# Query and key stacks transposed by DMA instead of by TensorE, in an attention and expert kernel on one Trainium2 core

## The reference

```
h = einsum('bhid,oi,od->bho', x, weighted_sum, weight)      # the mix: 512 x 256 per batch
h = h + attention(layernorm(h))                             # 16 heads of 16
h = h + experts(layernorm(h))                               # 8 dense experts, 256 -> 1024 -> 256, relu,
                                                            # weighted by sigmoid gates over 0.5
attention: q, k, v = split(t @ qkv_w.T + qkv_b); q, k = rotate(q), rotate(k)
           q = q / max(norm(q), 1e-12); k = k / max(norm(k), 1e-12)     # per head
           out = softmax(q k^T / 4) v;  return out @ out_w.T + out_b
```

## Time and profile before

| what | value |
|---|---|
| median of 3 runs | 2000.3 us (1999.42 to 2002.72) |
| the profiled execution, its own time | 1997.95 us |
| its span, first to last instruction | 1996.2 us |
| PE / ACT / DVE / POOL busy | 95% / 57% / 39% / 34% |
| mean granted TensorE clock | 0.975 of full speed |
| first stage, before the first `f1` (L862) | 133 us |
| body 0 / each of the bodies 1 to 6 / last experts | 291 / 233.4 / 171 us |

### The profile page before, as it was taken

The page is one execution under the profiler, slowest core; times in us unless marked ns, Lnnn a source line. Parts: engine busy times, 40 slices in busy tenths (PEclk is TensorE's granted clock), DMA queues, the critical chain, the costliest instruction groups (busy, mean ns, idle before and its releaser), DMA issues.

```text
span 1996.2 us, 32932 instructions
## 1 busy us (share of the span) xinstructions
PE 1889.2 (95%) x13120; PEld 1203.0 (60%) x13120; DVE 779.2 (39%) x1664; ACT 1128.6 (57%) x1713; POOL 676.5 (34%) x570
## 2 busy tenths in 40 slices
PE   5679898899999999999999999999999999999999
PEld 4236543577547764577646775467645776466666
DVE  6756933537203470145502472034800455022000
ACT  2644666544765467644765547654576446655444
POOL 1103422324323352333423343233433334234443
PEclk8679998899999999999999999999999999999999
DMA  4113332332112321131212321123211322113221
GB/s 157 31 60 117 103 134 85 127 138 85 64 64 106 107 74 64 66 136 64 85 64 93 109 84 65 64 106 97 84 64 64 127 75 85 64 64 117 106 85 54
DMA packets 40473, 176.65 MB, mean 88 GB/s; under 512 B 4072, under 2 KB 17152, under 8 KB 23936
## 3 DMA queue, kind: packets, MB, share of 16 engines
q1 hardware_dynamic: 40320, 174.54, 24.9%
HBM read 153.55 MB, written 20.97 MB: 87 GB/s over the span
## 4 chain that ended last, share of the span: by engine, by line
PE 78%; DVE 8%; issue 6%; ACT 2%; POOL 1%; POOLq 0%; DVEq 0%; ACTq 0%
PE bank_h L862 29%; PE bank_f L881 10%; PE bank_f L883 10%; PE bank_f L884 10%; PE bank_o L790 5%; PE bank_s L778 3%; PE bank_s L695 3%; PE bank_s L696 2%; PE bank_s L697 2%; PE bank_s L764 1%; DVE qk L984 1%; DVE tmp_b L979 1%; DVE y L902 1%; POOL hl L552 1%; PE bank_s L830 1%
## 5 line engine op out<-in xcount | busy, mean ns | idle before, releaser
L552 POOL TENSOR_TENSOR hl<-h,hh 128x512 f16<-128x512 f32 x512 | 608.7, 1189 | 1121.8 <-ACT hh L672 685.9
L862 PE MATMUL bank_h<-x,w1s 128*128 128x512 f16 x3072 | 757.1, 383 | 9.0 <-ACT hh L672 8.6
L669 ACT ACTIVATE h<-bank_h,b1s 128x512 f32<-128x512 f32 x512 | 352.3, 688 | 451.9 <-PE bank_h L862 442.6
L881 PE MATMUL bank_f<-w2s,hh 128*128 128x256 f16 x2048 | 562.9, 275 | 2.2 <-DVE acc L1089 2.0
L883 PE MATMUL bank_f<-w2s,hh 128*128 128x256 f16 x2048 | 561.1, 274 | 0.0
L884 PE MATMUL bank_f<-w2s,hl 128*128 128x256 f16 x2048 | 560.9, 274 | 0.0
L862 PEld LDWEIGHTS bank_h<-x,w1s 128*128 128x128 f16 x3072 | 288.6, 99 | 338.6 <-ACT hh L672 45.4
L672 ACT ACTIVATE hh<-bank_h,b1s 128x512 f16<-128x512 f32 x512 | 351.4, 686 | 0.0
L638 ACT ACTIVATE probs<-bank_s 128x1024 f32<-128x1024 f32 x240 | 246.9, 1029 | 157.7 <-PE bank_s L778 156.7
L881 PEld LDWEIGHTS bank_f<-w2s,hh 128*128 128x128 f16 x2048 | 202.1, 99 | 109.9 <-issue 42.9
L1089 DVE SCALAR_TENSOR_TENSOR acc<-bank_f,gw,acc 128x256 f32<-128x256 f32 x256 | 106.1, 476 | 365.3 <-PE bank_f L884 365.2
(11 more groups left out here) (141 smaller groups left out, 1709.6 us busy)
## 6 DMA issues: line engine op xcount, KB each, us to landing
w1s<-w_parts SPq DMA_DIRECT2D x56, 1024.0 KB, 4.8
w2s<-w_parts SPq DMA_DIRECT2D x56, 1024.0 KB, 4.8
xraw<-in_x_t_dram SPq DMA_DIRECT2D x32, 512.0 KB, 4.6
raw<-in_w_dram SPq DMA_DIRECT2D x16, 1024.0 KB, 6.7
w_parts<-w1s SPq DMA_DIRECT2D x8, 1024.0 KB, 8.8
w_parts<-w2s SPq DMA_DIRECT2D x8, 1024.0 KB, 10.7
out_dram<-acc SPq DMA_DIRECT2D x16, 256.0 KB, 6.1
raw<-in_qkv_w_t_dram SPq DMA_DIRECT2D x1, 768.0 KB, 7.1
```

The lines of the kernel that those rows point to most:

```text
L552: pool.tensor_tensor(hl[n % HBUFS][:], h32[n % 2][:], hh[n % HBUFS][:], ALU.subtract)\
L669: act.activation(h32[n % 2][:], bank_h[n % 2][:, :], ACT.Relu, bias=b1s[:, e, m:m + 1]).then_inc(h_hi.sem, 1)
L862: last = pe.matmul(bank_h[n % 2][:, :], w[:, wp, k, m * P:(m + 1) * P], x16s[fb % 2][:, xp, k, :], start=(k == 0 and wp + xp == 0), stop=( ...
L881: pe.matmul(o, high, w[:, 0, m, :], start=(m == 0 and t % 2 == 0), stop=False, skip_group_check=True)
```

## The change

The transposes leave PE. SP issues eight DMA transposes per batch, one for each tile and each of queries and keys, from `stack` straight into `qt` or `kt`. A second stack buffer lies in the unused half of `probs[1]`. A DMA transpose waits for its stack and for the landing of the same kind (`a`) of the tile before. The eight are issued behind the loads of expert 3 and ahead of those of expert 4 (in body 0: ahead of `load_raw(4)` and `store_parts(3)`). The steps `qk_turn`, ACT's copies from PSUM and the float16 identity go. `unit` and `stack` move from 17.1 and 18.6 (+ 1.5 per tile) to 19.1 and 19.4 (+ 0.9 per tile). The two chains of norms become one over 128 columns, at 15.7. The output bias moves on POOL from `qkv` 3 to a step of its own at 24.0. In the first stage all rotations come first, then the chain, then unit and stack of the four tiles in turn.

```diff
@@ attention_order
-                  (17.1 + 1.5 * t, "unit", t), (18.6 + 1.5 * t, "stack", t), (20 + 1.5 * t, "qk_turn", t)]
-    steps += [(6.8, "ln1", 0), (14.7, "qk_norm", 0), (19.2, "qk_norm", 1)]
+                  (UNIT[t], "unit", t), (UNIT[t] + 0.3, "stack", t)]
+    steps += [(6.8, "ln1", 0), (15.7, "qk_norm", 0), (24.0, "out_bias", 0)]
...
-        order = ["ln1_turn 0", "ln1_turn 1", "qkv 0", "rotate 0", "ln1_turn 2", "qkv 1", "rotate 1", "qk_norm 0",
-                 "unit 0", "ln1_turn 3", "qkv 2", "stack 0", "rotate 2", "unit 1", "qkv 3", "qk_turn 0", "stack 1",
-                 "rotate 3", "qk_norm 1", "qk_turn 1", "unit 2", "stack 2", "unit 3", "qk_turn 2", "stack 3",
-                 "qk_turn 3"]
+        order = ["ln1_turn 0", "ln1_turn 1", "qkv 0", "rotate 0", "ln1_turn 2", "qkv 1", "rotate 1", "ln1_turn 3",
+                 "qkv 2", "rotate 2", "qkv 3", "rotate 3", "qk_norm 0", "unit 0", "stack 0", "unit 1", "stack 1",
+                 "unit 2", "stack 2", "unit 3", "stack 3"]
...
+UNIT = [19.1, 20.0, 20.9, 21.8]
@@ build
+        stacks = [stack, probs[1][:, 2:4, :].rearrange("p j t -> p (j t)").bitcast(F16)
+                  .rearrange("p (a h s d) -> p a h s d", a=2, h=HEADS, s=4)]
...
+        stack_turned = [signal(f"stack_turned{a}", 16 * TT) for a in range(2)]
@@ sync
+            def turn_stacks(b, tiles):
+
+                for t in tiles:
+                    for a in range(2):
+                        wait(sp, stack_ready, b, 2 * t + a + 1)
+                        if t == 0:
+                            wait(sp, scored, b, 0)
+                        else:
+                            wait(sp, stack_turned[a], b, 16 * t)
+                        sp.dma_start_transpose((qt, kt)[a][:, :, t * P:(t + 1) * P],
+                                               stacks[t % 2][:, a].rearrange("p h s d -> p (h s d)"))\
+                          .then_inc(stack_turned[a].sem, 16)
...
                 for e in range(2, EXPERTS):
                     load_expert(b, e)
+                    if more and e == 3:
+                        turn_stacks(b + 1, range(TT))
@@ gpsimd
-                elif stage == "qkv" and n == TT - 1:
+                elif stage == "out_bias":
@@ scalar, stage "stack"
                     for a in range(2):
-                        wait(act, stack_turned, ab, 2 * (n - 1) + a + 1)
+                        wait(act, weighed, ab, 0)
+                        if n >= 2:
+                            wait(act, stack_turned[a], ab, 16 * (n - 1))
                         high, _, unit_qk = stack_slots(n, a)
                         copy(high, unit_qk).then_inc(stack_hi.sem, 1)
-                        if n:
-                            take_turned(n - 1, a, ab, fb is None)
-                elif stage == "qk_turn" and n == TT - 1:
-                    for a in range(2):
-                        take_turned(n, a, ab, fb is None)
@@ tensor
-                elif stage == "qk_turn":
...
-                        for h in range(HEADS // 2):
-                            last = pe.transpose(turned[:, h, :],
-                                                stack[:, a, 2 * h:2 * h + 2, :, :].rearrange("p h s d -> p (h s d)"),
-                                                ident16[:])
...
                     if n == 0:
-                        wait(pe, qt_out, ab, TT)
-                        wait(pe, kt_out, ab, TT)
+                        for turned in stack_turned:
+                            wait(pe, turned, ab, 16 * TT)
@@ vector, stage "unit"
                     wait(dve, weighed, ab, 0)
+                    if n >= 2:
+                        wait(dve, stack_ready, ab, 2 * (n - 1))
```

More of the change, by code:

```diff
@@ L216, in build @@
         ident = sb("ident", [P, P])
-        ident16 = sb("ident16", [P, P], F16)
         mix = sb("mix", [P, 2, XK, D], F32R)
@@ L343, in build @@
         stack_ready = signal("stack_ready", 2 * TT)
-        stack_turned = signal("stack_turned", 2 * TT)
-        qt_out = signal("qt_out", TT)
-        kt_out = signal("kt_out", TT)
+        stack_turned = [signal(f"stack_turned{a}", 16 * TT) for a in range(2)]
         scored = signal("scored", 4 * UNITS)
@@ L388, in qkv_banks @@
             return bank_h if alone and t % 2 else bank_s
-        def qk_turn_bank(a, alone):
-            return (bank_f if alone else bank_s)[a][:, :].bitcast(F16).rearrange("p (h t) -> p h t", t=P)
         def stack_slots(t, a):
-            high, low = ((stack[:, 0, :, 0:4:2, :], stack[:, 0, :, 1:4:2, :]) if a == 0 else
-                         (stack[:, 1, :, 0:2, :], stack[:, 1, :, 2:4, :]))
+            stack_t = stacks[t % 2]
+            high, low = ((stack_t[:, 0, :, 0:4:2, :], stack_t[:, 0, :, 1:4:2, :]) if a == 0 else
+                         (stack_t[:, 1, :, 0:2, :], stack_t[:, 1, :, 2:4, :]))
             values = units_at[:, t % 2, a * D:(a + 1) * D].rearrange("p (h d) -> p h d", d=HD)
@@ L509, in _ @@
             load_x(1, [0, 1])
+            turn_stacks(0, range(TT))
             load_raw(1)
@@ L515, in _ @@
             for e in range(2, EXPERTS):
+                if e == 3:
+                    turn_stacks(1, range(TT))
                 if e + 1 < EXPERTS:
@@ L577, in _ @@
             pool.wait_ge(consts_in, 16 * 8)
-            pool.tensor_copy(ident16[:], ident[:]).then_inc(pool_consts, 1)
             run(pool, steps)
@@ L584, in copy @@
                 return act.activation(out_ap, in_ap, ACT.Copy)
[L586 to L591, removed]
             def split_x(b, t):
@@ L753, in steps @@
                     last.then_inc(qkv_done.sem, 1)
-                elif stage == "qk_turn":
[L755 to L762, removed]
-                        for h in range(HEADS // 2):
-                            last = pe.transpose(turned[:, h, :],
-                                                stack[:, a, 2 * h:2 * h + 2, :, :].rearrange("p h s d -> p (h s d)"),
-                                                ident16[:])
-                        last.then_inc(stack_turned.sem, 1)
                 elif stage == "scores":
@@ L785, in steps @@
                         wait(pe, ln1_lo, ab, TT)
+                        if fb is None:
+                            pe.wait_ge(pool_consts, 1)
                     if tile == 0:
@@ L987, in steps @@
                 elif stage == "qk_norm":
-                    wait(dve, summed, ab, TT // 2 * (n + 1))
-                    cut = slice(n * TT * HEADS, (n + 1) * TT * HEADS)
-                    flat = ss[:].rearrange("p t h -> p (t h)")[:, cut]
+                    wait(dve, summed, ab, TT)
+                    flat = ss[:].rearrange("p t h -> p (t h)")
                     att_v.link(dve, dve.tensor_scalar(flat, flat, NORM_EPS * NORM_EPS, None, ALU.max))
-                    rsqrt(flat, cut)
+                    rsqrt(flat, slice(0, TT * 2 * HEADS))
                 elif stage == "unit":
                     wait(dve, weighed, ab, 0)
+                    if n >= 2:
+                        wait(dve, stack_ready, ab, 2 * (n - 1))
                     scale = y1[:, n * 2 * HEADS:(n + 1) * 2 * HEADS].unsqueeze(2)\
@@ L1006, in steps @@
                         wait(dve, stack_hi, ab, 2 * n + a + 1)
-                        wait(dve, stack_turned, ab, 2 * (n - 1) + a + 1)
+                        if n >= 2:
+                            wait(dve, stack_turned[a], ab, 16 * (n - 1))
                         dve.tensor_tensor(low, unit_qk, high, ALU.subtract).then_inc(stack_ready.sem, 1)
```

## The result

The changed kernel takes **1979.8 us** in the median of four runs (1977.8 to 1986.1) against 2000.8 us before: ratio 0.9897, 95% interval 0.9884 to 0.9909. 1971 had been forecast, in a range of 1953 to 2030, with 0.64 on faster. The profiled execution took 1980.74 us, 1979.0 of it span, 17.2 us less than the span before.

A forecast was written before the change was run, and what follows sets the result against it. PE was taken as the bound (busy 1889 of 1996 us). Six steady bodies (25 us), body 0 (4) and the first stage (0) gave 29 us off the 2000.3 us median: 1971 us, range 1953 to 2030.

The forecast's parts named there:

- What leaves PE: Steady bodies: the four groups of 16 transposes leave PE, with the idleness ahead of one, 4.2 us per body.
- The stall at chunk 18: Steady body: PE's 0.97 us wait for ACT, traced to POOL's bias stretching DVE's norm chain, counted as won.
- What is late next there is nothing: Chain of norms at 15.7: its result is first wanted by `unit` 0, 8 us later, so no cost.
- The landing: Before `scores` 0: landings of one kind follow each other; PE waits 4L - 13.1 us if positive, 0.9 us forecast.
- L: Time from the issue of one DMA transpose to its landing, put at 3.5 us.
- my own formula: Whole kernel: gain = 6 x (5.1 - max(0, 4L - 13.1)) + 4 + (14 - 4L), zero at L = 4.5.
- the rival with the landing hidden whole: At L up to 3.3 the bodies win 30.6 us; total 1957 to 1966 us; chance 0.22.
- The two estimates from the Trainium skill: DMA transpose: 3.0 us from fixed cost plus bandwidth; 10.5 us if 1309 ns added up over eight blocks.
- Body 0: Chunks 16 to 25, bound by DVE: PE's saving counts only in part, 4 us won.
- First stage: Bound by DVE: savings and losses leave the last landing at 77.5 us against 77.45 before, so nothing won.
- Units every 0.9 chunk: Steady bodies: ACT falls about 2 us behind PE under closer unit spacing, PE does not feel it; priced at nothing.

The follow-up runs named there:

- experiment 3: The kernel before with only the output bias moved on POOL to place 24.0: 1985.9 us, ratio 0.9920.
- experiment 4: The changed kernel with the output bias put back in POOL's step of qkv 3: 2003.5 us, ratio 1.0019.
- Experiment 5: The kernel before with the bias at 24.0, one chain of norms at 15.7 and first-stage rotations first; TensorE still transposes: 1996.2 us, ratio 0.9975.
- experiments 1 and 2: Changed kernel; 1: each transpose waits for the landing two tiles before, 1972.6 us; 2: each waits for the one just before, queries or keys alike, 2070.9 us.
- experiment 7: The changed kernel, but POOL's output bias waits until the last stack is ready: 1977.3 us, ratio 0.9892.
- experiment 6: The changed kernel with the norms in two chains of 64 columns again, at 14.7 and 15.7: 1997.0 us, ratio 0.9972.

## Why the prediction was right in sign and too high in size

21 us were won where 29 had been forecast. A steady body won 3.0 us instead of 4.2: PE's work fell by 4.1 in the mean, but its idleness rose by 1.1. By its steps:

- **What leaves PE**: right. 4.2 us were forecast; PE's busy time in body 3 falls by 4.2 us from the kernel before (231.5 to 227.35), and by 3.4 from the kernel with the bias moved (230.76).
- **The stall at chunk 18**: its cause was right, as experiment 3 shows, and its own price nearly so (1.13 us for 0.97). The moved bias was worth more than that stall: 2.1 us a body in the kernel before, and 24 us in all inside the change (1.0019 against 0.9897), where it would else meet `rotate` 3 (experiment 4).
- **"What is late next there is nothing"**: this step failed. I asked who wants the chain's result and found nobody for 8 us; I did not ask what stands behind the chain in DVE's list. That was the accumulation of expert 1, which I had taken at its old time, and it cost 1.14 us of idleness a body (1.36 from the start of `f1` 19 to that of `f1` 20). Experiment 5 shows it without any DMA.
- **The landing**: the mechanism, two chains of four landings, was right (experiments 1 and 2). L was 3.2 us and not 3.5 (one transpose alone took 3.1 where I had put 2.8, and the twin in flight adds about 0.1 and not 0.7), yet the wait was 1.8 us and not 0.9. The first keys' transpose went out 7.7 us after chunk 19 began (961.61 - 953.91) instead of 5.1. The late chain and accumulation had pushed `unit` 0 back, so that the keys' stack was ready at 6.6; the other 1.1 us are SP's, held by the issue of the queries' transpose (1.24 us), a term that my sum did not have. Farther on one issue held SP for 2.26 us.
- **Luck**: with 3.2 us in place of 3.5 my own formula gives a gain of 36 us, not 29, and the condition of the rival with the landing hidden whole (L up to 3.3) was met, but not its time. L put too high hid a part of what the steps left out. With the landings freed the bodies do take the 229.2 us of the forecast, by another road.
- **The two estimates from the Trainium skill**: the figures of the Trainium skill (DMA: Bandwidth & Descriptors, sections on the anatomy of one DMA and on latency), worked out to an estimate of 3.0 us, are near the measured 3.2, though its fixed 2.0 us was measured on DMAs issued from GpSimd and these are issued from SP. The sum of the 1309 ns of the Trainium skill (VectorE: DVE Perf Modes, The three transpose paths) over eight blocks is not: all eight blocks of 128x128 together land in 3.2 us.
- **Body 0**: 4 us forecast, 0.7 measured. PE's busy time falls by 6.9 us there and its idleness rises by 6.3. DVE's queue again: the waits at chunks 18 and 19 come to 4.31 us, all of it for the accumulation at chunk 19, and came to 4.07 before, so that nothing is won there; and at chunk 24 PE now waits 2.73 us for DVE's parts of expert 3.
- **First stage**: nothing forecast, 1.6 us lost. The 3.1 us credited to the moved bias were taken back in the main, 2.1 us, by its collision with `rotate` 3 (experiment 7). With the bias held the first scores start at 77.4 us, where 77.5 had been forecast.
- **Units every 0.9 chunk**, priced at nothing: right in the bodies; in the changed kernel's steady body PE has no wait for ACT between chunks 20 and 25.

## What to carry to other kernels

A change of several parts needs each part run alone: here all the rest (64 DMA transposes for 512 of TensorE, the later units, the one chain) nets nothing without a two-line move of a POOL addition. When an operation is put at a new place in an engine's list, look for what stands behind it and not only for who reads its result. A place in a list does not bind an engine that has nothing else to do: if it must not run early, it needs a wait.

## What the runs showed of the hardware

- A DMA transpose of 256 KB from SBUF to SBUF lands in 3.2 us in the median with two in flight (3.1 one at a time), but holds the issuing queue for 1.24 us, against 0.32 for a load of 1024 KB; 3 of the 64 held it for 1.9 to 2.3.
- A DVE operation that runs beside a POOL addition is stretched until that ends. The two multiplications of 3.86 us end at 57.58, the bias beside them at 57.30; the link of 2.30 us ends at 952.77, its bias at 952.69. Without the bias they take 1.72 and 0.23 us.
- A stall can cost more than its length. In experiment 4's body 3 PE stands still for 3.74 us, from 962.96 to 966.70; the granted clock falls to 0.50 (1.2 GHz) at 965.1, within the stall, and is back at 1.00 at 972.0, 5.3 us after it. Behind the stalls of 1.14 and 1.8 us in the changed kernel's bodies it stays at 1.00. The length alone does not decide: in experiment 6 the stall at chunk 19 is 2.6 us in all six bodies, and the clock falls in four of them.

```profile
963.00:965.10 2.10, 0.00 (x0) 0.00 (x0) 1.93 (x6) 1.27 (x2) 0.76 (x1) 1.00 0.83 335
965.20:966.70 1.50, 0.00 (x1) 0.03 (x1) 1.47 (x4) 0.00 (x0) 0.30 (x1) 0.50 0.43 175
966.70:971.90 5.20, 5.20 (x19) 2.73 (x20) 3.13 (x6) 1.15 (x2) 0.00 (x0) 0.50 0.26 50
972.00:976.00 4.00, 4.00 (x32) 2.92 (x31) 2.10 (x3) 3.57 (x6) 1.16 (x1) 1.00 0.35 66
```
